# Sums of squares in the state bank, a group's additions at the head of the next step, scores two groups behind

## What is computed

```python
x = x + mixer(xn) + ffn(xn)
# mixer: proj = xn @ in_proj_w.T, split into gate, hBC, dt
#   hBC = silu(conv4(hBC) + conv_b), split into hs (128 heads x 64), B, C (8 groups x 128 states)
#   per chunk of 128 tokens: Gm = C B^T, M = Gm * exp(segsum(A dt)), Y_diag = M (hs dt)
#   states carried over the 4 chunks with their decays, Y_off = (C state) * exp(A_cs)
#   xg = (Y_diag + Y_off + D hs) * silu(gate)
#   xg is divided by its root mean square over each of 8 groups of 1024 channels,
#   times norm_weight, then @ out_proj_w.T
```

## Time and profile before

| what | value |
|---|---|
| median of 3 runs | 1745.4 us (1744.01 to 1745.47) |
| the profiled execution's own time | 1747.96 us |
| its span, first to last instruction | 1746.2 us |
| TensorE busy | 1668.7 us, 96% of the span |
| VectorE busy | 1354.4 us, 78% |
| ScalarE busy | 1191.5 us, 68% |
| POOL busy | 1095.1 us, 63% |
| mean granted clock of TensorE | 0.981 |
| HBM traffic | 120 GB/s over the span |

### The profile page before, as it was taken

How to read it: one execution, slowest core, us unless ns; L and a number is a source line. 1 busy time by engine, 2 the same in 40 slices (tenths; PEclk the granted TensorE clock), 3 DMA queues, 4 the chain that set the end, 5 groups by cost and what they waited for, 6 DMA issues and landing times.

```text
span 1746.2 us, 28887 instructions
## 1 busy us (share of the span) xinstructions
PE 1668.7 (96%) x9694; PEld 1371.7 (79%) x9694; DVE 1354.4 (78%) x2388; ACT 1191.5 (68%) x2442; POOL 1095.1 (63%) x1384
## 2 busy tenths in 40 slices
PE   6889999999999999999898899999999999999997
PEld 5677878787888878788687688787878787888875
DVE  5777787878778787878878677878787878787785
ACT  2457777777777777777634577777767777777773
POOL 5235676667666766676663366676676667666764
PEclk9989999999999999999989899999999999999998
DMA  4133443344334434433222333443443344334431
GB/s 146 38 128 117 140 132 133 118 139 136 122 125 140 137 114 133 139 129 115 77 85 73 126 125 133 139 130 114 139 139 127 117 139 139 125 120 139 139 105 45
DMA packets 82146, 212.03 MB, mean 121 GB/s; under 512 B 11024, under 2 KB 27408, under 8 KB 81744
## 3 DMA queue, kind: packets, MB, share of 16 engines
q1 hardware_dynamic: 82000, 210.20, 36.8%
HBM read 207.01 MB, written 3.15 MB: 120 GB/s over the span
## 4 chain that ended last, share of the span: by engine, by line
PE 75%; DVE 15%; ACT 4%; issue 4%; DMA 0%; POOL 0%; SPq 0%; DVEq 0%; POOLq 0%; ACTq 0%
PE bh L505 20%; PE bg L505 18%; PE bo L662 15%; PE by L635 6%; DVE cv L691 5%; PE bt L627 4%; PE bt L649 4%; PE bt L671 2%; DVE acc L709 2%; ACT cv L282 2%; DVE mt L910 2%; PE bo L505 1%; DVE S L716 1%; DVE by L902 1%; PE bo L601 1%
## 5 line engine op out<-in xcount | busy, mean ns | idle before, releaser
L436 POOL TENSOR_TENSOR wl<-raw,wh 128x256 fp32r<-128x256 f32 x584 | 537.0, 950 | 131.8 <-ACT wh L278 131.8
L489 POOL TENSOR_TENSOR wol<-raw_o,woh 128x256 fp32r<-128x256 f32 x256 | 184.3, 741 | 487.0 <-ACT woh L403 487.0
L691 DVE SCALAR_TENSOR_TENSOR cv<-bh,par_sb,cv 128x511 f32<-128x511 f32 (+2 forms) x408 | 304.7, 747 | 197.1 <-ACT cv L282 192.0
L291 ACT ACTIVATE mt<-cs_row,cs_tok 128x128 f32<-128x128 f32 x1024 | 324.3, 389 | 0.0
L662 PE MATMUL bo<-woh,xh 128*128 128x512 f32 x512 | 212.5, 415 | 1.4 <-POOL xl L477 1.4
L662 PE MATMUL bo<-woh,xl 128*128 128x512 f32 x512 | 201.7, 394 | 0.0
L662 PE MATMUL bo<-wol,xh 128*128 128x512 f32 x512 | 199.9, 390 | 0.0
L364 ACT ACTIVATE xh<-xg 128x512 fp32r<-128x512 f32 x128 | 81.0, 633 | 162.8 <-DVE xg L906 162.8
L287 ACT ACTIVATE bh<-cv 128x512 f32<-128x512 f32 x136 | 81.8, 602 | 155.7 <-DVE cv L691 155.7
L477 POOL TENSOR_TENSOR xl<-xg,xh 128x256 fp32r<-128x256 f32 x256 | 181.7, 730 | 5.8 <-ACT xh L364 5.8
L894 DVE SCALAR_TENSOR_TENSOR sg<-tg,bg 128x512 f32<-128x512 f32 x128 | 87.9, 686 | 125.5 <-ACT tg L399 125.5
(11 more groups left out here) (159 smaller groups left out, 3351.0 us busy)
## 6 DMA issues: line engine op xcount, KB each, us to landing
raw<-in_w_step SPq DMA_DIRECT2D x128, 512.0 KB, 3.6
cs_row<-cs_rows SPq DMA_DIRECT2D x128, 512.0 KB, 4.4
raw_o<-in_w_out SPq DMA_DIRECT2D x128, 256.0 KB, 2.7
ec_row<-ec_rows SPq DMA_DIRECT2D x256, 96.0 KB, 3.7
raw<-in_w_bc SPq DMA_DIRECT2D x16, 512.0 KB, 3.7
acc<-in_x SPq DMA_DIRECT2D x2, 1024.0 KB, 5.7
mt<-in_w_ffn SPq DMA_DIRECT2D x2, 1024.0 KB, 6.7
out_dram<-acc SPq DMA_DIRECT2D x2, 1024.0 KB, 4.7
```

What stands on the lines that cost most here:

```text
L291: e = act.activation(mt[:, m % 2, h, chunk(j)], cs_row[:, m % 2, h, chunk(j)], ACT.Relu, bias=cs_tok[:, b, j, 2 * m + h:2 * m + h + 1], sc ...
L436: e = pool.tensor_tensor(wl[:, n % 2, part], raw[:, n % 2, part], wh[:, n % 2, part].bitcast(F32), ALU.subtract)
L489: e = pool.tensor_tensor(wol[:, 1 - u, part], raw_o[:, 1 - u, part], woh[:, 1 - u, part].bitcast(F32), ALU.subtract)
L691: dve.scalar_tensor_tensor(out=cv[:, u, k:], in0=src[:, 0:L - k], scalar=par_sb[:, un % UNITS, TAPS - 1 - k:TAPS - k], in1=cv[:, u, k:], o ...
```

## The change

- The sums of squares go from the end of m (behind the transposes, bank by) to the place between state read and output matmuls of the same m, into four columns of bank bt that the state read leaves free. They no longer wait for xg. The transposes of that m wait for the mean square.
- VectorE's mean square goes from the head of m+1 to the place behind sg at m. POOL's root goes from the head of m+1 to the place behind the output weights' low part at m.
- VectorE's four additions go from behind the D product at m+1 to the place behind xt and ahead of tap 1 at m+1.
- Scores, B transposes, masks and btok copies come two groups behind the projections instead of one; those of the last two groups come in step 0 of the step stage. VectorE's silu waits for the B transposes of two groups before. The group loop has 8 iterations instead of 9.
- At the start of the second batch the wait for the last mean square moves from g = 0 (bank by) to g = 1 (bank bt).

Core of the diff, for ScalarE first (`take_b` is the btok copy):

```diff
-                    if g >= 1:
-                        act.wait_ge(t_bt, did(b * GROUPS + g - 1))
-                        act.activation(btok[:, g - 1], bo[3][:, 0:NS * P].rearrange("p (c k) -> p c k", c=NS),
-                                       ACT.Copy).then_inc(a_bt, 1)
+                    if g >= 2:
+                        take_b(b, g - 2)
...
                         act.wait_ge(t_hs, did(n))
                         last_tap(un, u, bh)
+                        if m == 0:
+                            take_b(b, GROUPS - 2)
...
                         act.activation(tg[:, :], bg[:, :], ACT.Tanh, scale=0.5).then_inc(a_tg, 1)
+                        if m == 0:
+                            take_b(b, GROUPS - 1)
```

POOL:

```diff
-                    if m - 2 >= PER_GROUP and (m - 2) % PER_GROUP == 0:
-                        rms((n - 2) // PER_GROUP - 1)
...
                         e.then_inc(p_wol, 1)
+                    if m >= PER_GROUP and m < STEPS and (m - 2) % PER_GROUP == PER_GROUP - 1:
+                        rms((n - 2) // PER_GROUP)
                     if m + 2 < STEPS or (m < STEPS and b + 1 < NB):
                         split_lo(step(b, m + 2))
```

TensorE (the body of `scores` is that of lines 594 to 607):

```diff
+            def scores(b, g):
+                n, u = b * GROUPS + g, g % 2
+                if g == 0:
+                    pe.wait_ge(pv, b * PRO_DVE + PRO_DVE)
+                pe.wait_ge(v_h2, did(b * UNITS + 2 * g + 1))
+                pe.wait_ge(v_g, did(n - 1))
+                for j in range(NJ):
+                    mm = pe.matmul(bo[2][:, chunk(j)], h2[:, u, chunk(j)], ct[:, g, chunk(j)], start=True, stop=True)
+                mm.then_inc(t_gm, 1)
+                pe.wait_ge(a_bt, did(n - 1))
+                for c in range(NS):
+                    mm = pe.transpose(bo[3][:, chunk(c)], h2[:, u, chunk(c)], ident[:, :])
+                mm.then_inc(t_bt, 1)
...
+                    if g >= 2:
+                        scores(b, g - 2)
...
                         project(bh, b, step(b, m) % 2, 0).then_inc(t_hs, 1)
+                        if m == 0:
+                            scores(b, GROUPS - 2)
...
-                        if m - 1 >= PER_GROUP and (m - 3) % PER_GROUP == PER_GROUP - 1:
-                            pe.wait_ge(v_ms, did((n - 3) // PER_GROUP))
...
                         project(bg, b, step(b, m) % 2, 1).then_inc(t_g, 1)
+                        if m == 0:
+                            scores(b, GROUPS - 1)
...
                         mm.then_inc(t_off, 1)
+                    if has(m - 2) and (m - 2) % PER_GROUP == PER_GROUP - 1:
+                        pe.wait_ge(p_sqa, squares(b, m - 2))
+                        for j in range(NJ):
+                            mm = pe.matmul(bt[:, NS * P + j:NS * P + j + 1], sqa[:, chunk(j)], ones[:, 0:1],
+                                           start=True, stop=True)
+                        mm.then_inc(t_ss, 1)
...
                         pe.wait_ge(v_off, did(n - 1))
+                        if m >= PER_GROUP and (m - 2) % PER_GROUP == PER_GROUP - 1:
+                            pe.wait_ge(v_ms, did((n - 2) // PER_GROUP))
                         for j in range(NJ):
                             mm = pe.transpose(bt[:, chunk(j)], h2[:, u, chunk(j)], ident[:, :])
                         mm.then_inc(t_t, 1)
-                    if has(m - 2) and (m - 2) % PER_GROUP == PER_GROUP - 1:
-                        pe.wait_ge(p_sqa, squares(b, m - 2))
-                        pe.wait_ge(v_xg, did(min(n - 1, b * STEPS + STEPS - 1)))
-                        for j in range(NJ):
-                            mm = pe.matmul(by[:, j:j + 1], sqa[:, chunk(j)], ones[:, 0:1], start=True, stop=True)
-                        mm.then_inc(t_ss, 1)
```

VectorE (`mask_scores` is lines 841 to 845 with g in place of g - 1):

```diff
+                    if g >= 2:
+                        dve.wait_ge(t_bt, did(b * GROUPS + g - 2))
+                    silu_conv(un, 0, bank_b[g % 2], h2[:, g % 2, :])
+                    silu_conv(un + 1, 1, bank_c[g % 2], ct[:, g, :])
+                    if g >= 2:
+                        mask_scores(b, g - 2)
...
-                    if ended is not None:
-                        mean_square(ended)
...
                                           ALU.mult).then_inc(v_x, 1)
+                    if ended is not None:
+                        add_group(b, ended)
                     if has(m):
                         tap(un, u, bh, 1)
...
-                    if ended is not None:
-                        add_group(b, ended)
...
                         dve.wait_ge(t_t, did(n - 2))
+                        if m < 2:
+                            dve.wait_ge(t_bt, did(b * GROUPS + GROUPS - 2 + m))
+                        if m == 0:
+                            mask_scores(b, GROUPS - 2)
                         silu_conv(un, u, bh, h2[:, u, :])
...
                     if has(m - 1):
+                        if m >= PER_GROUP and (m - 2) % PER_GROUP == PER_GROUP - 1:
+                            mean_square((n - 2) // PER_GROUP)
                         dve.wait_ge(t_off, did(n - 1))
...
                         dve.tensor_tensor(xg[:, 1 - u, :], by[:, :], sg[:, 1 - u, :], ALU.mult).then_inc(v_xg, 1)
+                    if m == 0:
+                        mask_scores(b, GROUPS - 1)
```

More of the change, by code:

```diff
@@ L303, in split_ffn, with take_b @@
                 act.activation(whf[b], raw_f, ACT.Copy).then_inc(a_ffn, 1)
+            def take_b(b, g):
+                act.wait_ge(t_bt, did(b * GROUPS + g))
+                act.activation(btok[:, g], bo[3][:, 0:NS * P].rearrange("p (c k) -> p c k", c=NS),
+                               ACT.Copy).then_inc(a_bt, 1)
             for b in range(NB):
@@ L551, in _ @@
                     project_ag(0)
-                for g in range(GROUPS + 1):
-                    if g < GROUPS:
-                        pe.wait_ge(p_wl, did(bc(b, g)))
-                        if g == 0:
-                            pe.wait_ge(pa, b * PRO_ACT + ACT_ABS)
-                        elif g == 1:
-                            pe.wait_ge(v_off, did(b * STEPS - 1))
-                        else:
-                            pe.wait_ge(v_h2, did(b * UNITS + 2 * g - 4))
-                        project(bank_b[g % 2], b, bc(b, g) % 2, 0).then_inc(t_b, 1)
-                        if g == 0:
-                            pe.wait_ge(pa, b * PRO_ACT + ACT_AGC)
-                        elif g == 1:
-                            pe.wait_ge(pa, b * PRO_ACT + ACT_UT)
-                        elif g >= 2:
-                            pe.wait_ge(v_h2, did(b * UNITS + 2 * g - 3))
-                        project(bank_c[g % 2], b, bc(b, g) % 2, 1).then_inc(t_c, 1)
+                for g in range(GROUPS):
+                    pe.wait_ge(p_wl, did(bc(b, g)))
+                    if g == 0:
+                        pe.wait_ge(pa, b * PRO_ACT + ACT_ABS)
+                    elif g == 1:
+                        pe.wait_ge(v_off, did(b * STEPS - 1))
+                        pe.wait_ge(v_ms, did(b * GROUPS - 1))
+                    else:
+                        pe.wait_ge(v_h2, did(b * UNITS + 2 * g - 4))
+                    project(bank_b[g % 2], b, bc(b, g) % 2, 0).then_inc(t_b, 1)
+                    if g == 0:
+                        pe.wait_ge(pa, b * PRO_ACT + ACT_AGC)
+                    elif g == 1:
+                        pe.wait_ge(pa, b * PRO_ACT + ACT_UT)
+                    elif g >= 2:
+                        pe.wait_ge(v_h2, did(b * UNITS + 2 * g - 3))
+                    project(bank_c[g % 2], b, bc(b, g) % 2, 1).then_inc(t_c, 1)
                     if g == 0:
@@ L593, in _ @@
                         mm.then_inc(pe_, 1)
-                    if g >= 1:
-                        n, u = b * GROUPS + g - 1, (g - 1) % 2
-                        if g == 1:
-                            pe.wait_ge(pv, b * PRO_DVE + PRO_DVE)
-                        pe.wait_ge(v_h2, did(b * UNITS + 2 * g - 1))
-                        pe.wait_ge(v_g, did(n - 1))
-                        for j in range(NJ):
-                            mm = pe.matmul(bo[2][:, chunk(j)], h2[:, u, chunk(j)], ct[:, g - 1, chunk(j)],
-                                           start=True, stop=True)
-                        mm.then_inc(t_gm, 1)
-                        pe.wait_ge(a_bt, did(n - 1))
-                        for c in range(NS):
-                            mm = pe.transpose(bo[3][:, chunk(c)], h2[:, u, chunk(c)], ident[:, :])
-                        mm.then_inc(t_bt, 1)
+                    if g >= 2:
+                        scores(b, g - 2)
                 for m in range(STEPS + 2):
@@ L810, in decays_and_route, with mask_scores @@
                 assert done[b] == PRO_DVE_DTD
+            def mask_scores(b, g):
+                dve.wait_ge(t_gm, did(b * GROUPS + g))
+                dve.tensor_tensor(gt[:, g, :].rearrange("p (j c) -> p j c", j=NJ),
+                                  bo[2][:, :].rearrange("p (j c) -> p j c", j=NJ),
```

(12 more changed lines are left out.)

31 lines of the change are left out of this document (9 added, 22 removed).

## The result

The changed kernel takes **1695.97 us** (median of 4 runs, 1695.85 to 1696.18) against 1744.7 us (4 runs, 1742.6 to 1745.47): a ratio of 0.9723, 95% interval 0.9706 to 0.974. Forecast were 1697.6 us and a range of 1687 to 1712. The profiled executions are 1747.96 and 1696.02 us, 51.9 apart, where the sum said 47.8.

A forecast was written before the change was run, and what follows sets the result against it. TensorE was taken as the bound, busy 96% of the span; gains lay in its idle times and low-clock stretches. -17.6 - 31.6 + 1.05 + 0.4 = -47.8 gave 1700.2, less 2.6 for the median 1697.6 us; range 1687 to 1712.

The forecast's parts named there:

- The group's end: At 14 group ends inside the batches, earlier sums and additions save 1.26 us each, 17.6 us in all.
- The 1.0 us for the root: At a group's end, POOL needs 1.0 us for the reciprocal root, there by 231.9, before the additions start.
- The 0.49 us saved by the earlier sums: At a group's end, the next projection starts at 231.94 instead of 232.43, as sums no longer wait for xg.
- the 0.61 us of lateness: After a group's end, additions hold the first tap 0.61 us late, carried through to the state matmuls.
- The rival by which the additions come back in full at the next state matmuls: Group's end saves nothing, as the additions' delay of the first tap returns in full: 1715 us, chance 0.06.
- The price of the sums: At a group's end, eight passes of the sums of squares still cost 0.89 us on TensorE.
- The start of a batch: Low-rank matmuls to step 1's transposes: lagged scores save 15.8 us per batch, 31.6 in both.
- Mask waits of 1.2 and 1.5: In the group stage, TensorE newly waits 1.2 us for mask 0 and 1.5 us for mask 5.
- the 10.47 us: At a batch's start, step 1's transposes follow its projection by 10.47 us, from 113.1 to 123.6.
- The ping-pong rival: In the group stage, TensorE may wait for a mask at each hand-over through one bank: 1711 us, chance 0.12.
- The clock as the slower case: Short waits in the group stage keep the granted clock low there, 78 us more: 1776 us, chance 0.03.
- The ends of the batches: Sums ahead of the out matmuls wait for POOL: 1.05 us lost in batch 0, 0.4 in the last batch.

The follow-up runs named there:

- before_again: The kernel before the change, unchanged, run once more for its profile: 1742.56 us.
- no_early_adds: Changed kernel with VectorE's four additions back behind the D product; sums, mean square and root stay early: 1710.88 us.
- sums_twice: Changed kernel with each group's four sum matmuls issued twice, the second four overwriting the same values: 1709.24 us.
- less_vector: Changed kernel with the third convolution tap for B and C of groups 2 to 7 on 8 columns only, leaving out the rest: 1695.02 us.
- end_sums_last: Changed kernel with the sums behind the output matmuls in the last iteration of each batch: 1693.75 us.
- no_early_sums: Changed kernel with sums, mean square and root back where they stood before; only the additions are early: 1724.32 us.
- group_end_only: Kernel before with only the group's end changed (sums, mean square, root, additions early); scores stay one group behind: 1721.59 us.
- group_stage_only: Kernel before with only the scores moved to two groups behind; sums, mean square, root and additions as before: 1716.5 us.

## Why the prediction was right

**The direction and the size.** Inside the batches the steps stand as forecast: waits gone where they were said to go, waits new where they were said to come. The landing within 1.6 us of the median is in part luck. Against the profiled executions the sum was 4.1 us too small, and 2.4 of these are the chance at the start. Then 2.6 us were taken off because the profiled execution before lay above the median of its kernel; the changed kernel's profiled execution lies within 0.1 of its own median, so that this step had no ground in the change and happened to bring the number nearer. And part of the stage's gain belongs to the execution that the forecast was read from: `before_again`, 5.4 us shorter than the first profile, has 5.7 us less in its two stages.

**The group's end** (forecast 1.26, measured 1.44 per end). Sums without a wait, 0.89 us of passes, additions without a wait for the root, a tap late by part of VectorE's idle time: all shown. The 1.0 us for the root had no row in the group that the prediction names; it takes 1.03 after. The 0.49 us saved by the earlier sums came out as 0.50 (transposes at 201.51 to projection at 214.05, against 219.39 to 232.43). The term that was mis-sized is the 0.61 us of lateness, 0.43 measured. It assumed that mt keeps its 1.37 us; it takes 1.22 in all 14 steps where POOL's root runs beside its start, and 1.37 to 1.40 in nearly all where the weight split does. That POOL's work slows this operation is an inference from these rows and wasn't tried. The rival by which the additions come back in full at the next state matmuls is out: `no_early_adds` is 14.9 us slower.

**The price of the sums.** The rows said 0.89 us for eight passes. `sums_twice` bears them out: 0.89 us more for eight more. Each pass has a weight load of its own, and these take as long; the loads of after and of `sums_twice`:

```profile
209.95 0.97 PEld L662 LDWEIGHTS bt<-ones,sqa 128*128 128x128 f32 x8
212.49 1.87 PEld L662 LDWEIGHTS bt<-ones,sqa 128*128 128x128 f32 x16
```

That the load sets the interval of 0.11 us is read from these rows; one-column matmuls without a new load were not tried. The Trainium skill (TensorE: Matmul & The Clock Gate, "Wait — 56ns, not 53.3ns?") has a floor of about 25 ns between small matmuls, by which eight passes would be an estimated 0.2 us. The trace doesn't refute the floor, but it is not what bounds these passes.

**The start of a batch** (forecast 15.8, measured 15.5 and 15.6). Mask waits of 1.2 and 1.5 were forecast, 1.0 and 1.3 measured. The 1.7 us that step 1's transposes wait for yo are inside the 10.47 us that were forecast from that step's projection, and these came out as they stand (111.13 to 121.60). The projection itself came 0.4 us late although the mask waits were 0.4 shorter, so the terms between were 0.8 too small. Right for this pair of profiles; what I didn't see is that 2.7 to 3.0 us per batch hang on the clock of the particular execution of before. The ping-pong rival at every group didn't happen. VectorE nevertheless holds part of the stage: made lighter in `less_vector`, it gives back 1.5 us per batch.

**The clock as the slower case** is out: with waits of 1.0, 1.3 and 1.7 us in the stage the granted clock stayed at 1.00 in every window shown. The Trainium skill (TensorE: Matmul & The Clock Gate, "A second HAM failure mode: psum-queue depth-cycling") tells of frequent short idle moments that made the clock swing. In this stage the trace doesn't show that: its waits are three in 67 us, and the clock didn't move.

**The ends of the batches** are the part that went wrong. In batch 0 the delay by the wait for POOL was near the forecast: the first small matmuls of the next batch (`project_ag`, 128x68) start 16.40 us behind step 63's transposes instead of 15.20, so +1.20 where 1.05 was forecast. But from there to the low-rank matmuls it takes 30.92 us instead of 32.67, and so the stretch is 0.55 shorter and not 1.05 longer. In both kernels the clock falls in this place with TensorE busy all the time, but it stays low for a shorter time after the change. The two windows of before, then the two of after:

```profile
884.00:886.00 2.00, 2.00 (x19) 2.00 (x20) 2.00 (x1) 0.49 (x1) 0.00 (x0) 0.98 0.03 8
886.00:896.00 10.00, 10.00 (x41) 9.32 (x41) 9.62 (x13) 1.34 (x2) 7.74 (x7) 0.50 0.00 0
```

```profile
857.00:861.00 4.00, 4.00 (x36) 3.92 (x34) 3.86 (x6) 0.00 (x0) 0.63 (x1) 0.98 0.02 4
861.00:867.00 6.00, 6.00 (x24) 5.42 (x24) 5.79 (x7) 1.34 (x2) 6.00 (x6) 0.50 0.00 0
```

The prediction passed the delay on unchanged "to everything up to the next scores", as if the clock behind it stayed as it was. What the wait has to do with the shorter low stretch stays open, but it repeats: the whole stretch takes 47.3 us in six profiles with the sums ahead there (46.8 in `sums_twice`), 47.8 in three with the old order in bank by, and 48.3 in the fourth, `no_early_sums`, where the ffn matmuls wait 1.8 us for the additions.

In the tail the sum took 0.4 and left out "another 1 to 2 us" for the clock. The clock did fall. The table shows +2.20; set against `end_sums_last`, whose clock was the same up to there, the order of the sums costs 3.4. Together the two ends came out as forecast, +1.65 against +1.45, only because the two errors, 1.6 us too much and 1.8 too little, nearly cancel: luck, and not a reading.

## What to carry to other kernels

When a reduction over an accumulated buffer is put ahead of other work in an in-order queue, look at the ends of the loop by themselves: inside the loop its input was 1.8 us early, at the end it was 2.75 us late, and had a burst at the lower clock behind it. Move a consumer early together with what it waits for: the additions alone cost 0.68 us per group, the sums, mean square and root alone gained 0.41, and all together gained 1.44. And before a difference is assigned to a change, compare two profiles of the same kernel. Between two profiles of the kernel before, the group stage differed by 2.7 and 3.0 us; between two of the changed kernel, the start differed by 2.2 and batch 0's group ends by 1.2, while batch 1's and the tail agreed to 0.2.

## What the runs showed of the hardware that I had not expected

- The same waits don't always cost the same. Behind the same 4.05 us wait the first four matmuls of the projection held TensorE for 1.86 us (start to start of the next four) in one execution and 1.31 in another. Behind a wait of 2.4 to 2.5 us at the end of batch 1 the 16 matmuls of Y_diag took 1.96 to 1.98 us in six profiles and 1.09 in seven, in either order of the sums.
- The lower clock also came with TensorE busy all the time. In the stretch that no kernel changed, 28 to 36 us, the mean granted clock was anything from 0.57 to 1.00; at the end of batch 0 it was 0.50 for ten microseconds before the change and for six after it.
- The kernel before varied by 9 us over its runs (1739.5 to 1748.5), the changed one by 0.3 within its four and by 1.3 over five. The group stage's part in this is shown: 79.8 to 82.8 us with the long waits, 67.15 to 67.25 without. That these waits make the whole time vary is not: over four runs each, `group_end_only`, which has them, varied by 2.9 us, and `group_stage_only`, which hasn't, by 3.2.
- VectorE's product over 128x1024 took 1.22 us in each of the 14 steps where POOL computed the root beside it, and 1.37 to 1.40 in nearly all the steps where POOL split weights (both in the changed kernel).
